# The first turn of the cross attention takes query tiles into the places of its missing output tiles, and the first keys are split sooner

## The chip, the cores and the metric

The kernel runs on one core of a Trainium2 chip. The metric is the device time of one execution in microseconds (us). Engines are named as the profile names them: PE is TensorE's matmul side (PEld its weight load), DVE is VectorE, ACT is ScalarE, POOL is GpSimd, SP is SyncE, which issues all DMAs here.

## The reference

One decoder layer on x (2 x 256 rows of 512) with a context (2 x 512 rows of 512): a causal self attention of 32 heads, a cross attention of 32 query heads over 8 key heads, and a permuted feed forward. The middle part is what the change touches:

```python
def _L0_xattn_ref(latents, context, Wq, Wk, Wv, Wo, q_norm_w, k_norm_w):
    kv = jnp.concatenate([context, latents], axis=1)
    q = (latents @ Wq).reshape(bsz, q_len, HEADS, HEAD_DIM).transpose(0, 2, 1, 3)
    k = (kv @ Wk).reshape(bsz, kv_len, KV_HEADS, HEAD_DIM).transpose(0, 2, 1, 3)
    v = (kv @ Wv).reshape(bsz, kv_len, KV_HEADS, HEAD_DIM).transpose(0, 2, 1, 3)
    q = rms_norm(q, q_norm_w)
    k = rms_norm(k, k_norm_w)
    qg = q.reshape(bsz, KV_HEADS, groups, q_len, HEAD_DIM)
    scores = jnp.einsum('bhgqd,bhkd->bhgqk', qg, k) * scale
    probs = jax.nn.softmax(scores.astype(jnp.float32), axis=-1).astype(q.dtype)
    out = jnp.einsum('bhgqk,bhkd->bhgqd', probs, v)
    ...
    return out @ Wo
x = _layernorm(x + _L0_attn_ref(x, ...), axis=-1)
x = _layernorm(x + _L0_xattn_ref(x, ctx_4096, ...), axis=-1)
x = _layernorm(x + _L0_ffn_ref(x, ...), axis=-1)
```

## The kernel before

Every product is made in three passes (`three_passes`): each operand is split into a rounded high part and the remainder, the low part, and hi x hi, hi x lo and lo x hi are added in one PSUM bank. Splitting a tile is therefore a copy (hi, mostly on ACT) and a difference (lo, on DVE or POOL), and both are awaited before the product.

**Stage 1, `self_attention_and_keys`.** The self attention and the keys and values of the cross attention, interleaved. `order_of_work` writes one list, ORDER, and every engine goes through it and does its own share of each entry. An engine never overtakes itself, so the list sets each engine's order. Entries that matter here: ("part", (n, r)) is an eighth of the key and value work for row tile n (12 of them); ("KT"/"KX") transposes of its keys and their way out; ("Q", a) is query tile a of head 0 (PE: 12 products, ACT: copy q_rows, DVE: four sums of squares); ("QT", a) its transpose and split; ("QM", (half, step)) the scale of two query tiles (step 0: mean on DVE, power on POOL; step 1: q_rms on DVE); ("W", 9) the split of the query weights of the next head, in four pieces; ("KS", 0) the split of head 0's first keys, in two halves; ("XS", j) score tile j of the first unit (PE), ("XM", j) its maximum (DVE), ("XE", j) its exponential (ACT), ("XI", j) 1 / sum (DVE) and the norm of the probabilities (POOL). XS 0 waits for both halves of KS.

**Stage 2, `cross_attention`.** Eight turns, one for each key head: the first one, five in a loop, and the last two written out. A turn has four segments s = 0 to 3. In segment s the engines work on unit s's probabilities (two batches x two pairs of query groups) and on the scores of the next unit: six transposed probability tiles T 0 to 5 (PE), split on ACT and DVE, six products with the values (O), four score tiles S with maximum M, exponential E, 1/sum I and POOL's norm. `Turn.tensor_order`, `scalar_order` and `vector_order` write a segment out, and each has four places f[0] to f[3] for fillers: query tiles Q of the next head, transposed query tiles QT, output tiles W of a finished head. On PE, f[0] and f[1] stand between T 1 and T 2, f[2] and f[3] between O 3 and O 4. T, Q, QT and W use three PSUM banks in rotation (4, 5, 6): a tile may only start when the tile three uses earlier has been taken out by DVE (`ring_free`). The table FILLERS says what stands where. In the first turn there is no finished head, so `fillers` drops the W entries of segment 0 (`from_before`), and two of its places are empty. In the last turn (LAST_FILLERS) no Q is left. POOL does the norms and the splits of keys, values and weights in the order of `body`; T 0 of a segment needs the norm of all four tiles of its unit.

Of the kernel before, what the change touches and what calls it, by code (L numbers as in the profile page):

```python
# [52 lines left out]
def f32(ap):  # L53
    return ap.bitcast(F32)
# [27 lines left out]
def order_of_work():  # L82
# [73 lines left out]
    order += [("Q", 2), ("QT", 1)]  # L156
# [3 lines left out]
    order += [("W", 9), ("QM", (1, 0))]  # L160
    parts(1)
    order.append(("KS", 0))
    parts(1)
    for j in range(UT):
        order.append(("XS", j))
        parts(1)
        if j == 0:
            order.append(("QM", (1, 1)))
        order.append(("XM", j))
        if j > 0:  # L170
            order.append(("XI", j - 1))
        order.append(("XE", j))
# [10 lines left out]
def self_attention_and_keys(nc, d, k):  # L183

    with ExitStack() as ctx:
# [165 lines left out]
        def _(pool):  # L351
# [44 lines left out]
            for what, a in ORDER:  # L396
# [22 lines left out]
                elif what == "W" and a == 9:  # L419
                    for i in range(KT):  # L420
                        pool.wait_ge(w_his, KT * a + i + 1)
                        nc.gpsimd.tensor_tensor(k.wq_lo[:, i, :], w_raw[:, i, :], f32(k.wq_hi[:, i, :]), ALU.subtract)\
                            .then_inc(k.wq_split, 1)
                elif what == "XI":
                    pool.wait_ge(k.rinv_made, a + 1)
                    nc.gpsimd.tensor_scalar(k.prob[:, a, :], k.prob[:, a, :], k.rinv[:, a:a + 1], 1.0, ALU.mult, ALU.mult)\
                        .then_inc(k.prob_made, 1)
                elif what == "LN":
                    pool.wait_ge(var_made, a + 1)
                    nc.gpsimd.tensor_tensor(rstd[:, a:a + 1], var[:, a:a + 1], minus_half[:, 0:1], ALU.pow)\  # L430
                        .then_inc(rstd_made, 1)

        @block.scalar
        def _(act):
# [75 lines left out]
            for what, a in ORDER:  # L510
# [13 lines left out]
                elif what == "W":  # L524
# [6 lines left out]
                    if a == 9:  # L531
                        act.wait_ge(q_ps, TT)
                    for i in range(KT):
                        weights_hi(a, i)
                elif what == "A":
# [412 lines left out]

LAST_FILLERS = ((("W", 2), ("QT", 2), ("QT", 3), None),
# [5 lines left out]
class Turn:  # L955
# [25 lines left out]
    def fillers(self, s):  # L981
        kept = []
        for f in (FILLERS if self.more else LAST_FILLERS)[s]:
# [39 lines left out]
def cross_attention(nc, d, k):  # L1023
# [7 lines left out]
    with ExitStack() as ctx:  # L1031
# [126 lines left out]
        def _(pool):  # L1158
# [46 lines left out]
            def body(turn):  # L1205
# [7 lines left out]
                if turn.first:  # L1213
                    norms(0, (0, 1))
                    keys(1, 0, 0, 0)
                    norms(0, (2,))
                    keys(1, 1, 0, 1)
                    norms(0, (3,))
# [23 lines left out]
                if turn.more:  # L1242
# [5 lines left out]
                    if turn.ahead:  # L1248
                        wait_alone(ring_full, turn.use[3, "Q", 3] + 1)
                        query_weights(0, i + 2, c + 12)  # L1250
# [615 lines left out]
```

## Time and profile before

| | us |
|---|---|
| median of 3 runs (865.48 to 865.60) | 865.54 |
| the profiled execution | 865.81 |
| its span, first to last instruction | 864.0 |
| busy in the span: PE / PEld | 828.4 / 696.8 |
| busy in the span: DVE / ACT / POOL | 548.3 / 475.1 / 524.4 |
| mean granted clock of TensorE | 0.991 of full speed |

The profiled execution is one of its own and its span begins and ends at instructions; 1.8 us lie around it. A time on the trace is counted from the start of the span. Stage 1 ends at about 287, the first turn of stage 2 runs from there to 354.5, and the last turn's segments 1 and 2 lie around 777 to 806. In a timeline a row's second number is the length of an instruction, or of a run of like ones (x4). Products are pipelined: the next may start before the length shown has gone by. A bracket at a row's end gives how long the engine stood idle before it and who released it.

### The profile page before, as it was taken

To read this page: it belongs to the slowest core of one execution; us is meant where nothing else is said; L and a number is where in the kernel's file an instruction comes from. 1 tells how busy PE (TensorE), PEld (TensorE's weight loads), DVE (VectorE), ACT (ScalarE), POOL (GpSimd) and SP (SyncE) were. 2 spreads that over 40 slices of the span, in tenths; PEclk is the share of its full clock that TensorE was granted. 3 is DMA by queue.
4 is the path that set the end of the run, shared out by engine and by line. 5 is a ranking of instruction groups with operands and counts; after the bars stand their busy time and mean duration, and the time that the engine had idled before them with its cause. 6 is when DMAs were issued, how large, how long until landed. Compare 5 with 4: busy or idle time off the path is not lost. (4 is left out here: it accounts for less than half of the span.)

```text
span 864.0 us, 15103 instructions
## 1 busy us (share of the span) xinstructions
PE 828.4 (96%) x4841; PEld 696.8 (81%) x4841; DVE 548.3 (63%) x1505; ACT 475.1 (55%) x1006; POOL 524.4 (61%) x676
## 2 busy tenths in 40 slices
PE   7999999899999899999999999999999999999976
PEld 5777777677887688888888888888888888888763
DVE  4376665656445667767676776667677767767543
ACT  5666663565345645555555555556555545555363
POOL 3576873676425476666756756775775676446831
PEclk9999999999999999999999999999999999999998
DMA  7604222121141532102112121121121102000011
GB/s 225 185 30 134 63 87 94 53 74 50 49 135 50 170 103 87 50 20 86 46 40 67 36 67 67 36 67 67 36 67 67 36 11 71 1 0 2 0 25 49
DMA packets 48510, 56.22 MB, mean 65 GB/s; under 512 B 4670, under 2 KB 29772, under 8 KB 48460
## 3 DMA queue, kind: packets, MB, share of 16 engines
q1 hardware_dynamic: 48460, 55.59, 20.9%
q8 instruction: 27, 0.44, 0.2%
q14 instruction: 23, 0.19, 0.1%
HBM read 41.95 MB, written 13.63 MB: 64 GB/s over the span
## 5 line engine op out<-in xcount | busy, mean ns | idle before, releaser
L1202 POOL TENSOR_SCALAR prob<-prob,x_rinv 128x768 f32<-128x768 f32 x124 | 113.1, 912 | 175.7 <-DVE x_rinv L1368 175.7
L1310 ACT ACTIVATE pT_hi<-bank 128x512 fp32r<-128x512 f32 x192 | 114.4, 598 | 93.8 <-PE bank L1500 92.7
L1293 ACT ACTIVATE prob<-bank,x_nm,q_rms 128x768 f32<-128x768 f32 x124 | 123.3, 994 | 46.1 <-DVE x_nm L1362 45.8
L1402 DVE TENSOR_TENSOR pT_lo<-bank,pT_hi 128x512 fp32r<-128x512 f32 x192 | 130.3, 680 | 6.9 <-ACT pT_hi L1310 5.4
L1359 DVE TENSOR_REDUCE x_mx<-bank 128x1 f32<-128x768 f32 x124 | 118.3, 954 | 22.8 <-PE bank L1463 22.4
L1500 PE MATMUL bank<-ident,prob 128*128 128x128 f32 x768 | 115.7, 273 | 4.3 <-POOL prob L1202 2.9
L1500 PEld LDWEIGHTS bank<-ident,prob 128*128 128x128 f32 x768 | 95.1, 141 | 16.6 <-POOL prob L1202 3.6
L48 PE MATMUL bank<-pT_hi,xv_hi 128*128 128x512 f32 x192 | 86.5, 450 | 0.9 <-DVE pT_lo L1402 0.8
L448 ACT ACTIVATE s_self<-s_self,nm_self 128x128 f32<-128x128 f32 (+1 forms) x128 | 57.0, 447 | 54.2 <-DVE nm_self L588 54.0
L50 PE MATMUL bank<-pT_hi,xv_lo 128*128 128x512 f32 x192 | 75.7, 394 | 0.0
L49 PE MATMUL bank<-pT_lo,xv_hi 128*128 128x512 f32 x192 | 75.2, 392 | 0.0
L1463 PE MATMUL bank<-xk_hi,qT_hi 128*128 128x384 f32 x244 | 66.0, 352 | 1.1 <-ACT prob L1293 1.0
L1463 PE MATMUL bank<-xk_lo,qT_hi 128*128 128x384 f32 x244 | 63.2, 340 | 0.0
L1463 PE MATMUL bank<-xk_hi,qT_lo 128*128 128x384 f32 x244 | 62.9, 338 | 0.0
L48 PE MATMUL bank<-wq_hi,x_hi 128*128 128x512 f32 x144 | 58.5, 406 | 0.0
L48 PE MATMUL bank<-w_hi,cT_hi 128*128 128x512 f32 x128 | 56.0, 438 | 1.2 <-DVE x_rows L672 1.2
L1319 ACT ACTIVATE oT_hi<-bank 128x512 fp32r<-128x512 f32 x32 | 19.2, 598 | 68.9 <-PE bank L50 68.9
L50 PE MATMUL bank<-wq_hi,x_lo 128*128 128x512 f32 x144 | 56.4, 392 | 0.0
L49 PE MATMUL bank<-wq_lo,x_hi 128*128 128x512 f32 x144 | 56.4, 391 | 0.0
L603 DVE COPY pT_self<-bank 128x384 f32<-128x384 f32 x64 | 35.3, 552 | 30.7 <-PE bank L810 30.5
L48 PE MATMUL bank<-wo_hi,oT_hi 128*128 128x512 f32 x128 | 51.9, 406 | 0.0
L1463 PEld LDWEIGHTS bank<-xk_hi,qT_hi 128*128 128x128 f32 x244 | 43.8, 190 | 9.8 <-ACT prob L1293 2.0
(216 smaller groups left out, 2050.3 us busy)
## 6 DMA issues: line engine op xcount, KB each, us to landing
wo_raw<-in_Wo SPq DMA_DIRECT2D x8, 1024.0 KB, 5.5
v_by_head<-v_st SPq DMA_DIRECT2D x12, 512.0 KB, 3.3
kT_by_head<-kT_st SPq DMA_DIRECT2D x12, 512.0 KB, 3.2
xk_raw<-kT_by_head SPq DMA_DIRECT2D x16, 384.0 KB, 3.2
xv_raw<-v_by_head SPq DMA_DIRECT2D x16, 384.0 KB, 3.2
wq_raw<-in_Wq SPq DMA_DIRECT2D x6, 1024.0 KB, 5.4
wq_raw<-in_w_attn SPq DMA_DIRECT2D x12, 256.0 KB, 3.9
xk_raw<-in_ctx SPq DMA_DIRECT2D x8, 256.0 KB, 2.6
```

The lines of the kernel that those rows point to most:

```text
L48: nc.tensor.matmul(out, a_hi, b_hi, start=first, stop=False)
L49: nc.tensor.matmul(out, a_hi, b_lo, start=False, stop=False)
L50: return nc.tensor.matmul(out, a_lo, b_hi, start=False, stop=last)
L448: nc.scalar.activation(s_sb[:, c % 2, i, a:e], s_sb[:, c % 2, i, a:e], ACT.Exp, bias=nm[:, c % 2, i, qt:qt + 1], scale=-1.0, accum_out=rsu ...
L603: nc.vector.tensor_copy(pT[:, c % 2, i, :], bank[:, bank_of("T", (c, i)), 0:3 * P]).then_inc(pt_out, 1)
L1202: nc.gpsimd.tensor_scalar(prob[:, s, :], prob[:, s, :], rinv[:, s:s + 1], 1.0, ALU.mult, ALU.mult)\
L1293: nc.scalar.activation(prob[:, s, :].rearrange("p (a e) -> p a e", a=2), bank[:, at:at + 2, 0:HALF], ACT.Exp, bias=nm[:, s:s + 1], scale=q ...
L1310: nc.scalar.activation(pT_hi[:, a, :], bank[:, turn.bank[s, what, a], :], ACT.Copy)\
L1359: nc.vector.reduce_max(mx[:, s:s + 1], bank[:, at:at + 2, 0:HALF], AX.XY)\
L1402: nc.vector.tensor_tensor(pT_lo[:, a, :], bank[:, turn.bank[s, what, a], :], f32(pT_hi[:, a, :]), ALU.subtract).then_inc(ring_out, 1)
L1463: last = nc.tensor.matmul(bank[:, at + c, 0:HALF], a_hi[:, g, w], k_part[:, b, c * HALF:(c + 1) * HALF], start=start, stop=stop)
L1500: last = nc.tensor.transpose(bank[:, at, j * P:(j + 1) * P], prob[:, UT * (s % 2) + j, a * P:(a + 1) * P], ident[:])
```

## The change

Three things are moved; no work is added or removed.

1. In ORDER, ("KS", 0) goes from behind the weights to behind ("QT", 1). ("W", 9) becomes eight entries: ("WH", i), ACT's copy of piece i, and ("WL", i), POOL's difference of piece i, spread over the following parts. ("QM", (1, 0)) stands ahead of them.
2. The first turn gets a table of its own, FIRST_FILLERS. Q 0 and Q 1 go to segment 0, Q 2 to segment 1, Q 3 to segment 2; the last place of segment 1 and the first of segment 3 become empty.
3. In the first turn POOL splits the keys of the second batch directly behind the first norm and does the other three norms after them.

```diff
@@ order_of_work
-    order += [("Q", 2), ("QT", 1)]
+    order += [("Q", 2), ("QT", 1), ("KS", 0)]
     parts(1)
     order += [("Q", 3), ("QM", (0, 1))]
     parts(1)
-    order += [("W", 9), ("QM", (1, 0))]
+    order += [("QM", (1, 0)), ("WH", 0), ("WH", 1)]
     parts(1)
-    order.append(("KS", 0))
+    order += [("WH", 2), ("WL", 0), ("WL", 1), ("WH", 3)]
     parts(1)
     for j in range(UT):
         order.append(("XS", j))
         parts(1)
         if j == 0:
-            order.append(("QM", (1, 1)))
+            order += [("QM", (1, 1)), ("WL", 2), ("WL", 3)]
@@ the first turn's table
+FIRST_FILLERS = ((("Q", 0), ("QT", 2), ("QT", 3), ("Q", 1)),
+                 (("Q", 2), None, None, None),
+                 (("Q", 3), ("QT", 0), ("QT", 1), ("W", 0)),
+                 (None, None, None, ("W", 1)))
...
-        for f in (FILLERS if self.more else LAST_FILLERS)[s]:
+        for f in (FIRST_FILLERS if self.first else FILLERS if self.more else LAST_FILLERS)[s]:
@@ POOL's body of a turn
                 if turn.first:
-                    norms(0, (0, 1))
+                    norms(0, (0,))
                     keys(1, 0, 0, 0)
-                    norms(0, (2,))
                     keys(1, 1, 0, 1)
-                    norms(0, (3,))
+                    norms(0, (1, 2, 3))
                     values(1, 0, i, c)
...
-                        wait_alone(ring_full, turn.use[3, "Q", 3] + 1)
+                        wait_alone(ring_full, turn.use[2 if turn.first else 3, "Q", 3] + 1)
```

**ScalarE near the end of stage 1**, from the copy of query tile 3 (q_rows) on; xk_hi is KS, wq_hi the weights, v_st, kT_st, k_rows and k_sq the parts of rows 10 and 11. Before:

```order
L546 ACTIVATE q_rows<-bank 128x512
L470 ACTIVATE v_st<-bank 128x512
L437 ACTIVATE wq_hi<-wq_raw 128x512 x4
L462 ACTIVATE kT_st<-bank,nw 128x512
L555 ACTIVATE xk_hi<-xk_raw0 128x384 x2
L478 ACTIVATE k_rows<-bank 128x512
L483 ACTIVATE k_sq<-k_rows 128x512
L462 ACTIVATE kT_st<-bank,nw 128x512
L560 ACTIVATE prob,x_rsum<-bank,x_nm,q_rms 128x768
```

After:

```order
L549 ACTIVATE qT_hi<-bank 128x4x128
L555 ACTIVATE xk_hi<-xk_raw0 128x384 x2
L546 ACTIVATE q_rows<-bank 128x512
L469 ACTIVATE v_st<-bank 128x512
L436 ACTIVATE wq_hi<-wq_raw 128x512 x2
L461 ACTIVATE kT_st<-bank,nw 128x512
L436 ACTIVATE wq_hi<-wq_raw 128x512 x2
L477 ACTIVATE k_rows<-bank 128x512
L482 ACTIVATE k_sq<-k_rows 128x512
```

The two halves of xk_hi moved ahead of the copy of query tile 3 and of the weights, and the weights stand in two pairs.

**GpSimd at the same place**: q_inv is the power of QM, wq_lo the weights, k_inv and k_rows the key norm of a part, prob the first norm of probabilities. Before:

```order
L422 TENSOR_TENSOR wq_lo<-wq_raw,wq_hi 128x512 x4
L418 TENSOR_TENSOR q_inv<-q_ms,minus_half 128x8
L411 TENSOR_TENSOR k_inv<-k_ms,minus_half 128x4
L413 TENSOR_TENSOR k_rows<-k_rows,k_inv 128x512
L426 TENSOR_SCALAR prob<-prob,x_rinv 128x768
```

After:

```order
L418 TENSOR_TENSOR q_inv<-q_ms,minus_half 128x8
L421 TENSOR_TENSOR wq_lo<-wq_raw,wq_hi 128x512 x2
L411 TENSOR_TENSOR k_inv<-k_ms,minus_half 128x4
L413 TENSOR_TENSOR k_rows<-k_rows,k_inv 128x512
L421 TENSOR_TENSOR wq_lo<-wq_raw,wq_hi 128x512 x2
L425 TENSOR_SCALAR prob<-prob,x_rinv 128x768
```

The power q_inv moved ahead of the weights, and two of the four weight pieces stand behind the key norm.

**ScalarE at the start of the first turn**, from the first two transposed tiles (pT_hi) to the output of segment 0 (oT_hi). Before:

```order
L1310 ACTIVATE pT_hi<-bank 128x512 x2
L1293 ACTIVATE prob,x_rsum<-bank,x_nm,q_rms 128x768
L1286 ACTIVATE qT_hi<-bank 128x4x128
L1310 ACTIVATE pT_hi<-bank 128x512 x2
L1293 ACTIVATE prob,x_rsum<-bank,x_nm,q_rms 128x768
L1310 ACTIVATE pT_hi<-bank 128x512
L1293 ACTIVATE prob,x_rsum<-bank,x_nm,q_rms 128x768
L1310 ACTIVATE pT_hi<-bank 128x512
L1293 ACTIVATE prob,x_rsum<-bank,x_nm,q_rms 128x768
L1286 ACTIVATE qT_hi<-bank 128x4x128
L1319 ACTIVATE oT_hi<-bank 128x2x256
```

After:

```order
L1313 ACTIVATE pT_hi<-bank 128x512 x2
L1296 ACTIVATE prob,x_rsum<-bank,x_nm,q_rms 128x768
L1285 ACTIVATE q_rows<-bank 128x512
L1289 ACTIVATE qT_hi<-bank 128x4x128
L1313 ACTIVATE pT_hi<-bank 128x512 x2
L1296 ACTIVATE prob,x_rsum<-bank,x_nm,q_rms 128x768
L1313 ACTIVATE pT_hi<-bank 128x512
L1296 ACTIVATE prob,x_rsum<-bank,x_nm,q_rms 128x768
L1313 ACTIVATE pT_hi<-bank 128x512
L1296 ACTIVATE prob,x_rsum<-bank,x_nm,q_rms 128x768
L1289 ACTIVATE qT_hi<-bank 128x4x128
L1285 ACTIVATE q_rows<-bank 128x512
```

Query tile 0 (q_rows) now stands behind the first exponential and ahead of QT 2 (qT_hi), query tile 1 ahead of oT_hi. VectorE's sums of squares stand in the same places.

**GpSimd in segment 0 of the first turn.** Before:

```order
L1202 TENSOR_SCALAR prob<-prob,x_rinv 128x768 x2
L1172 TENSOR_SCALAR xk_hi<-xk_raw1 128x384
L1174 TENSOR_TENSOR xk_lo<-xk_raw1,xk_hi 128x384
L1202 TENSOR_SCALAR prob<-prob,x_rinv 128x768
L1172 TENSOR_SCALAR xk_hi<-xk_raw1 128x384
L1174 TENSOR_TENSOR xk_lo<-xk_raw1,xk_hi 128x384
L1202 TENSOR_SCALAR prob<-prob,x_rinv 128x768
```

After:

```order
L1206 TENSOR_SCALAR prob<-prob,x_rinv 128x768
L1176 TENSOR_SCALAR xk_hi<-xk_raw1 128x384
L1178 TENSOR_TENSOR xk_lo<-xk_raw1,xk_hi 128x384
L1176 TENSOR_SCALAR xk_hi<-xk_raw1 128x384
L1178 TENSOR_TENSOR xk_lo<-xk_raw1,xk_hi 128x384
L1206 TENSOR_SCALAR prob<-prob,x_rinv 128x768 x3
```

The two key pieces now stand directly behind the first norm and ahead of the other three.

## Rows read from the trace of the kernel before

**Rows 1.** TensorE's timeline before the first score tile: start us, length us, engine, line

```profile
268.65 0.40 PE L50 MATMUL bank<-w_hi,x_lo 128*128 128x512 f32 x1
...
270.87 0.59 PE L926 MATMUL bank<-xk_hi,qT_hi 128*128 128x384 f32 x2 [1.82 <-issue]
```

**Rows 2.** Windows: busy us of PE, PEld, DVE, ACT, POOL; granted clock; DMA

```profile
272.00:276.00 4.00, 4.00 (x15) 3.41 (x14) 1.34 (x3) 1.70 (x4) 3.52 (x3) 0.58 0.29 92
...
303.00:307.00 4.00, 4.00 (x16) 3.71 (x16) 2.20 (x4) 1.57 (x3) 3.75 (x6) 0.61 0.94 331
...
791.00:796.00 5.00, 4.57 (x31) 4.13 (x30) 3.22 (x6) 3.08 (x6) 2.69 (x3) 1.00 0.00 0
```

**Rows 3.** Timelines of four engines around the first keys; their load's landing

```profile
252.11 0.35 SPq L341 DMA_DIRECT2D xk_raw<-kT_by_head  x1
...
DMA to landing us min/median/max: 3.2/3.2/3.2
...
264.49 0.60 ACT L546 ACTIVATE q_rows<-bank 128x512 f32<-128x512 f32 x1 [3.48 <-PE bank L50]
...
268.11 0.94 ACT L555 ACTIVATE xk_hi<-xk_raw 128x384 fp32r<-128x384 f32 x2
...
269.57 0.63 ACT L483 ACTIVATE k_sq<-k_rows 128x512 f32<-128x512 f32 x1
...
266.17 5.74 POOL L422 TENSOR_TENSOR wq_lo<-wq_raw,wq_hi 128x512 fp32r<-128x512 f32 x4 [6.65 <-ACT wq_hi L437]
...
268.67 2.10 DVE L707 TENSOR_TENSOR xk_lo<-xk_raw,xk_hi 128x384 fp32r<-128x384 f32 x2 [2.33 <-ACT xk_hi L555]
```

**Rows 4.** TensorE's timeline in segment 0 of the first turn

```profile
288.48 0.60 PE L1453 MATMUL bank<-ident,q_rows 128*128 128x128 f32 x4
...
289.80 0.66 PE L1500 MATMUL bank<-ident,prob 128*128 128x128 f32 x4 [0.72 <-DVE pT_lo L1402]
...
291.51 0.66 PE L1500 MATMUL bank<-ident,prob 128*128 128x128 f32 x4 [0.36 <-DVE pT_lo L1402]
...
296.07 0.62 PE L1463 MATMUL bank<-xk_hi,qT_hi 128*128 128x384 f32 x2 [1.02 <-ACT prob L1293]
...
302.74 0.48 PE L1500 MATMUL bank<-ident,prob 128*128 128x128 f32 x1 [2.04 <-POOL prob L1202]
```

**Rows 5.** Timelines: ScalarE in segment 0, VectorE's sums in segment 1

```profile
290.89 0.99 ACT L1293 ACTIVATE prob<-bank,x_nm,q_rms 128x768 f32<-128x768 f32 x1 [1.43 <-DVE x_nm L1362]
...
309.54 0.29 DVE L1333 CUSTOM_DVE_ANT_0 q_sq<-bank,q_rows 128x128 f32<-128x128 f32 x1 [1.74 <-ACT q_rows L1282]
...
310.38 0.08 DVE L1333 DVE_READ_ACCUMULATOR2_ANT q_ss<- 128x1 f32 x1
```

**Rows 6.** Timelines of SyncE and GpSimd in segment 0 of the first turn

```profile
290.11 0.35 SPq L1104 DMA_DIRECT2D xk_raw<-kT_by_head  x1
...
298.34 1.01 POOL L1174 TENSOR_TENSOR xk_lo<-xk_raw,xk_hi 128x384 fp32r<-128x384 f32 x1
...
301.78 0.91 POOL L1202 TENSOR_SCALAR prob<-prob,x_rinv 128x768 f32<-128x768 f32 x1
```

**Rows 7.** TensorE's timeline in segments 1 and 2 of the last turn

```profile
786.95 0.52 PE L1463 MATMUL bank<-xk_hi,qT_hi 128*128 128x384 f32 x2
...
791.87 0.33 PE L1500 MATMUL bank<-ident,prob 128*128 128x128 f32 x1 [0.43 <-POOL prob L1202]
...
799.29 0.61 PE L1463 MATMUL bank<-xk_hi,qT_hi 128*128 128x384 f32 x2
```

**Rows 8.** TensorE's timeline in segment 3 of the first turn

```profile
337.95 0.60 PE L1500 MATMUL bank<-ident,prob 128*128 128x128 f32 x4
...
339.80 0.48 PE L48 MATMUL bank<-wq_hi,x_hi 128*128 128x512 f32 x1
...
342.64 0.60 PE L1500 MATMUL bank<-ident,prob 128*128 128x128 f32 x4
...
348.15 0.52 PE L1463 MATMUL bank<-xk_hi,qT_hi 128*128 128x384 f32 x2
```

More of the change, by code:

```diff
@@ L418, in _ @@
                     nc.gpsimd.tensor_tensor(k.q_inv[:, w], k.q_ms[:, w], minus_half[:, w], ALU.pow).then_inc(k.first_inv, 1)
[L419 to L423, printed above, removed]
+                elif what == "WL":
+                    pool.wait_ge(w_his, KT * 9 + a + 1)
+                    nc.gpsimd.tensor_tensor(k.wq_lo[:, a, :], w_raw[:, a, :], f32(k.wq_hi[:, a, :]), ALU.subtract)\
+                        .then_inc(k.wq_split, 1)
                 elif what == "XI":
@@ L530, in _ @@
                         act.wait_ge(y_ps, TT)
-                    if a == 9:
-                        act.wait_ge(q_ps, TT)
                     for i in range(KT):
                         weights_hi(a, i)
+                elif what == "WH":
+                    act.wait_ge(q_ps, TT)
+                    weights_hi(9, a)
                 elif what == "A":
```

## The prediction, made before the changed kernel was run

> **What bounds the kernel now.** I read the granted clock and busy shares first, then TensorE's own list of waits, then its timeline around each wait, and then the timelines of the engines that release it. TensorE is the bound: it is busy without a gap through the middle turns of the second stage, so a microsecond of TensorE time that is saved ahead of them arrives at the end whole. The places where it stands still and that the change touches are two. At the end of the first stage it waits once, before the first score tile XS 0, from 268.65 + 0.23 = 268.88 (a 512-wide product starts every 0.23 us though it is shown 0.39 long) to 270.87, which is 1.99 us [rows 1]. In the first turn of the cross attention it waits four times: 0.72, 0.36, 1.02 and 2.04 us in the brackets [rows 4]. A bracket counts from the modelled end of the instruction ahead, so the loss is larger by its tail (0.25, 0.16, 0.16 and 0.13): 0.97, 0.52, 1.18 and 2.17, in sum 4.84 us. Behind the two longest waits the clock was half: 0.58 granted over 272 to 276 and 0.61 over 303 to 307, which costs 4 x 0.42 = 1.7 and 4 x 0.39 = 1.6 us [rows 2]. So 1.99 + 1.7 + 4.84 + 1.6 = 10.1 us are at stake, and no product, transpose or copy is added or taken away.
>
> **Part 1, the first keys are split earlier.** XS 0 waits for two halves of the key split. ScalarE did its two copies (0.94 us) at 268.11, behind four copies of the query weights; VectorE took 2.10 us for the two differences from 268.67 to 270.77 and TensorE started 0.10 later [rows 1, 3]. In the change the pair stands behind the split of query tile QT 1. Are the keys there? Their load was issued at 252.11 and took 3.2 us, so they lie in the buffer at 255.3 [rows 3]. Is there room? ScalarE sat idle for 3.48 us until 264.49 [rows 3], from 261.0, and 0.94 us fit; VectorE, idle as long before the sums of Q 3, can do its part by 263.2 (at 0.56 each, the length of the faster one in the 2.10) or 264.0 (at 2.10). Both are 5 us ahead of 268.88, so the 1.99 us go. GpSimd was busy from 266.17 for 5.74 us with the weights' low parts, beside which the 2.10 fell [rows 3].
> The Trainium skill, page "SBUF — State Buffer", section on contention of the shared port pair, says that a VectorE operation with two SBUF inputs and a GpSimd operation block each other for a whole instruction; the 2.10 us for a pair agree with it, and by it the pair would take 1.1 at its new place, where GpSimd is idle. Both values leave the sum as it is.
>
> What is late next? XS 1 follows XS 0 after one part of row 11, XS 2 needs the first exponential. VectorE first has to finish the row's sum of squares, whose squares ScalarE writes until 270.2 [rows 3] (so about 271.1), and the query scale, for which GpSimd's power now stands ahead of the weights and ends at 268. The maximum of XS 0 then runs at 271.3, its exponential at 272.6, and with 1.1 us from an exponential's start to the released product (0.99 for itself [rows 5], 0.1 to be seen) XS 2 may start at 273.7; TensorE comes there at 274.2. So 0.5 us is left, and a small miss costs tenths. On GpSimd the weight pieces WL 0 and 1 end at 270.5, the key norm of part 3 at 273.2, WL 2 and 3 (1.3 each) at 275.8, the first probability norm at 276.7 and the key norm of part 5 at 278.9, with TensorE asking for it at about 280.9. The weights are wanted only in the second stage. I cost all of this at nothing; without this cover WL 2 and 3 would cost up to 2.6. With no wait the clock should stay whole: it fell behind the two waits of about 2 us and was 1.00 around one of 0.43 in the last turn [rows 2, 7]. Part 1 gives 1.99 + 1.7 = **3.7 us**, with 1.9 as the low end (the clock falls anyway).
>
> **Part 2, query tiles in the places left empty in segment 0.** A query tile is 12 products, 342.64 - 339.80 = 2.84 us [rows 8]. Q 0 now stands between the second and third transposed tile of segment 0, Q 1 at its end. I follow it on the clock of the trace before, from the same entry. T 0 and T 1 end at 288.48; Q 0 runs to 291.3, QT 2 to 291.65. T 2 needs T 1's bank, free at 291.45, and starts at once: the waits of 0.97 and 0.52 go. T 3 now needs the bank of Q 0. ScalarE copies Q 0 behind the exponential (290.89 to 291.9) until 292.5, and VectorE's four sums of squares follow: from 309.54 they took until 310.47 [rows 5], 0.93 us, and begin 0.64 us after the copy's start. So Q 0's bank is free at 293.45, and TensorE, through with O 0 at 292.75, waits **0.7**. The next score tile behind the exponentials waits about **0.1** in place of 1.18, since the query tile has filled the time. Then Q 1 stands ahead of O 4 and O 5: segment 1 begins at 303.8, or 16.2 us after its entry. GpSimd by then has done one norm, two key pieces and three norms; the last exponential's sum is ready at about 300.8, its norm (0.91) at 301.8 [rows 6]. The 2.17 and the 1.6 of half clock go. Segments 0 and 1 lost 4.84 + 1.6 = 6.4 us, and now lose 0.8.
>
> **Part 3, what the later segments lose.** Q 2 keeps a place in segment 1 and Q 3 one in segment 2; the end of segment 1 and the front of segment 3 are empty. The trace shows both holes in its last turn, which has them by its own table. End of segment: from the last score tile at 786.95 to the fourth transpose at 791.87 it was 4.92 us, where the same work in segment 0, without its wait and its query transposes (0.35), took 302.74 - 296.07 - 2.17 - 0.35 = 4.15 and began 0.1 slow behind a wait of its own [rows 4]. So 4.92 - 4.05 = **0.9** is lost; the clock stayed whole [rows 2, 7]. The bracket alone (0.43 and a tail of 0.13) is the low end, 0.6. Front of segment 3: in the last turn the last score tile came 799.29 - 791.87 = 7.42 us after the fourth transpose, against 348.15 - 337.95 - 2.84 - 0.26 = 7.10 in segment 3 itself, less its query tile and three transposes [rows 7, 8]: 0.3 is the low end. In turn 0 the query scale stands ahead of T 0's difference on VectorE, and the second maximum stands behind the third tile's difference. The nearest row from above is the wait of 1.18 for such an exponential in segment 0 [rows 4]. I take **0.9**, since this wait has the same chain of VectorE and ScalarE. What follows, one output tile, covers the segment's last norm.
>
> The first turn now loses 0.7 + 0.1 + 0.9 + 0.9 = 2.6 instead of 6.4: **3.8 us** gained (3.0 to 4.5). Loads move with the GpSimd work that frees their buffers; every buffer is asked for later than that. The next turn's query weights no longer wait for Q 3 in segment 3, and GpSimd ends them some 5.8 us after that turn begins, 11 us before it needs a norm.
>
> **The sum.** The profiled execution took 865.81 us, its span is 864.0, so 1.8 lie around it. 864.0 - 3.7 - 3.8 = 856.5, and with 1.8 it is 858.3. The median of the three runs is 0.27 below the profiled run: **858.1 us**, a ratio of 0.991.
>
> **The rivals.**
> - *Half clock comes back elsewhere.* Waits of 0.7, 0.9 and 0.9 remain, and everything behind moves by 7.5 us against the clock's own course. Two rows at half clock cost 1.6 to 1.7 each [rows 2]. One gives 859.8, two 861.4. Against it: the wait of segment 1's kind left the clock at 1.00 [rows 2]. Chance 0.14.
> - *A new chain eats the first stage's gain.* If XS 2 or the key norms behind WL 2 and 3 come late, up to 2.6 of the 3.7 returns: 860.7. For it: only 0.5 us of room at XS 2. Chance 0.06.
> - *The holes only move.* If the two emptied places cost what segment 0 lost (1.18 and 2.17) and the new bank wait for Q 0 is 1.5, the first turn loses 4.9 + 1.6 of half clock and gains nothing: 858.1 + 3.8 = 861.9. The last turn speaks against it [rows 7]. Chance 0.05.
> - *Early keys aren't early.* Had their load landed after 262, ScalarE would stand at the copy with Q 3 and the row's values behind it. They lie there at 255.3 [rows 3]; then nothing of part 1 is gained, 861.8. Chance 0.01.
> - *Slower than before.* GpSimd now waits for head 0's second keys ahead of norms 1 to 3. Two pieces (0.5 + 1.01 each) and three norms of 0.91 make 5.8 us [rows 6], and segment 1 wants the last norm at 303.8, so each microsecond that the load lands after 298.0 goes to the end. It eats the whole gain from 298.0 + 7.5 = 305.5. Such a load took 3.2 us [rows 3] and here is issued at 290.11 [rows 6]. At 308 it would give 865.5 + 2.5 and half clock behind it, 869.7. Chance 0.02.
>
> **How the numbers follow.** The forecast has 0.72, its own range 856.6 to 859.5 from the bounds 3.0 to 4.5 and tenths at XS 2. The range of 856.2 to 861.6 leaves out about 0.1. A difference of 0.2% (1.7 us) is what a measurement of this kernel can tell from none, so the bounds are 863.8 and 867.3: faster 0.94 (forecast, half clock, chain, holes, with a little taken off for several at once), same 0.04, slower 0.02.
>
> **What would show it.** No wait before XS 0 and a granted clock of 1.00 from 268 to 287; the second stage beginning 3.7 us earlier (about 283.9); a wait of some 0.5 in the bracket before the fourth transposed tile of segment 0, on VectorE's sum of squares; none at segment 1's first transposes; one of 0.4 at segment 2's on GpSimd's norm, and short ones in segment 3 on VectorE or ScalarE; segment to segment, 16.2, 14.9, 17.4 and 14.6 us; the second turn beginning at about 347. A clock below 1.00 in the first turn, or a wait of over 1.5 us anywhere in it, would make it wrong.

## The result, and the profile of the changed kernel

| us | before | changed |
|---|---|---|
| median of 5 runs each | 865.60 (865.48 to 866.25) | 861.36 (859.09 to 861.86) |
| ratio, with its 95% interval | | 0.9939 (0.9916 to 0.9962) |
| the profiled execution | 865.81 | 861.36 |
| its span | 864.0 | 859.5 |
| PE busy in the span | 828.4 | 828.3 |
| first product of the columns (start of the program) | 13.98 | 15.31 |
| XS 0 could start | 268.88 | 271.81 |
| second stage begins | 287.57 | 286.82 |
| second turn begins | 354.45 | 349.93 |

The change gained 4.2 us where 7.4 were forecast; 861.36 lies inside the range of 856.2 to 861.6, 0.24 below its upper end. The surprise is in the last rows of the table: the changed places gave what was forecast, and 2.93 us were already lost before the first of them, in a part of the program that is the same in both kernels.

TensorE's timeline of the changed kernel at the end of the first stage (start us, length us, engine, line; the last row is the entry of the second stage):

```profile
271.81 0.51 PE L926 MATMUL bank<-xk_hi,qT_hi 128*128 128x384 f32 x2
...
274.68 0.51 PE L926 MATMUL bank<-xk_hi,qT_hi 128*128 128x384 f32 x2
...
277.10 0.51 PE L926 MATMUL bank<-xk_hi,qT_hi 128*128 128x384 f32 x2
...
286.82 1.06 PE L1503 MATMUL bank<-ident,prob 128*128 128x128 f32 x8 [0.32 <-PEq L185]
```

No bracket stands at XS 0 to 2. From XS 0 to the entry it is 15.01 us, against 18.69 of before from where XS 0 could start. That is 3.68 of the 3.7 of part 1. The two halves of the keys, in the timelines of ScalarE, VectorE and GpSimd, with the first exponential:

```profile
263.80 0.94 ACT L555 ACTIVATE xk_hi<-xk_raw 128x384 fp32r<-128x384 f32 x2
...
264.92 1.02 DVE L707 TENSOR_TENSOR xk_lo<-xk_raw,xk_hi 128x384 fp32r<-128x384 f32 x2
...
273.61 0.96 DVE L712 TENSOR_REDUCE x_mx<-bank 128x1 f32<-128x768 f32 x1
...
274.86 0.99 ACT L560 ACTIVATE prob<-bank,x_nm,q_rms 128x768 f32<-128x768 f32 x1 [0.68 <-DVE x_nm L714]
...
269.34 1.64 POOL L418 TENSOR_TENSOR q_inv<-q_ms,minus_half 128x8 f32<-128x8 f32 x1 [6.91 <-DVE q_ms L698]
```

VectorE's pair of differences took 1.02 us where GpSimd was idle (it is idle for the 6.91 us ahead of q_inv); in [rows 3] it took 2.10 beside GpSimd's weights. By the Trainium skill, page "SBUF — State Buffer", on the shared port pair, the two engines block each other for a whole instruction there; both durations agree with it.

The first turn, TensorE's timeline, all its rows that have a bracket after the entry, and the starts of segments 1 and 3 and of the second turn (x4 of L1503 with no bracket at 303.03, 335.29 and 349.93):

```profile
292.73 0.66 PE L1503 MATMUL bank<-ident,prob 128*128 128x128 f32 x4 [0.53 <-DVE q_ss L1336]
...
303.03 0.60 PE L1503 MATMUL bank<-ident,prob 128*128 128x128 f32 x4
...
318.14 0.33 PE L1503 MATMUL bank<-ident,prob 128*128 128x128 f32 x1 [0.43 <-POOL prob L1206]
...
335.29 0.60 PE L1503 MATMUL bank<-ident,prob 128*128 128x128 f32 x4
...
343.55 0.61 PE L1466 MATMUL bank<-xk_hi,qT_hi 128*128 128x384 f32 x2 [0.26 <-ACT prob L1296]
...
349.93 0.60 PE L1503 MATMUL bank<-ident,prob 128*128 128x128 f32 x4
```

The four brackets of [rows 4] (0.72, 0.36, 1.02, 2.04) are gone, and three shorter ones stand there. The turn takes 349.93 - 286.82 = 63.11 us, against 354.45 - 287.57 = 66.88 before. GpSimd has done the last norm of segment 0 in good time, although the second keys stand ahead of it:

```profile
292.67 0.51 POOL L1176 TENSOR_SCALAR xk_hi<-xk_raw 128x384 fp32r<-128x384 f32 x1 [0.17 <-DMA xk_raw<-kT_by_head]
...
300.19 0.91 POOL L1206 TENSOR_SCALAR prob<-prob,x_rinv 128x768 f32<-128x768 f32 x1 [0.33 <-DVE x_rinv L1371]
```

Windows (columns as in [rows 2]; the granted clock is the third number from the end) of the changed kernel: the end of the first stage, the first turn, and the place of [rows 2]'s second row:

```profile
268.00:287.00 19.00, 18.68 (x100) 16.34 (x99) 9.22 (x29) 12.36 (x24) 14.31 (x13) 1.00 0.28 84
287.00:349.00 62.00, 60.50 (x336) 52.01 (x335) 45.81 (x118) 37.19 (x69) 40.97 (x48) 1.00 0.36 117
303.00:307.00 4.00, 4.00 (x24) 3.58 (x23) 3.86 (x10) 2.06 (x4) 3.75 (x6) 1.00 0.36 98
```

**Where 2.9 us went.** The first product of the columns (L766) starts 1.33 us later than before. Up to there TensorE's products run at half pace (0.63 long, one every 0.43 us) until 12.4 in the kernel before and until 15.2 in the changed one. Of the 1.33 us, 0.2 are there at the first of these products (9.93 against 9.72) and 1.1 come from the longer stretch at half pace. This is the same product in the two timelines, of before and of the changed kernel:

```profile
12.42 0.47 PE L48 MATMUL bank<-x_hi,w_hi 128*128 128x512 f32 x1
```

```profile
12.62 0.63 PE L48 MATMUL bank<-x_hi,w_hi 128*128 128x512 f32 x1
```

Then, at 164 to 166, TensorE waits for VectorE's difference of x, as it does before. These are the rows of the changed kernel, and its windows there:

```profile
165.81 1.08 PE L839 MATMUL bank<-ident,k_rows 128*128 128x128 f32 x4 [1.78 <-DVE x_lo L681]
```

```profile
166.00:168.00 2.00, 2.00 (x8) 1.71 (x8) 0.93 (x5) 1.56 (x5) 1.59 (x4) 0.50 0.59 184
168.00:170.00 2.00, 2.00 (x20) 1.17 (x18) 0.00 (x0) 0.57 (x1) 1.83 (x6) 0.70 0.00 0
```

And those of the kernel before:

```profile
164.44 0.63 PE L839 MATMUL bank<-ident,k_rows 128*128 128x128 f32 x4 [1.78 <-DVE x_lo L681]
```

```profile
166.00:168.00 2.00, 2.00 (x38) 1.13 (x41) 0.78 (x5) 1.72 (x3) 1.83 (x6) 1.00 0.00 0
168.00:170.00 2.00, 2.00 (x27) 1.41 (x19) 0.48 (x1) 1.35 (x5) 1.83 (x6) 1.00 0.00 0
```

The wait is the same 1.78 us. Behind it the clock is at its lower level (0.50 is 1.2 of 2.4 GHz) in one and whole in the other, and from the transposes of x ahead of it (L898) to the second key transposes behind it (L839) it is 10.99 us against 9.39. So 1.3 and 1.6 of the 7.45 us that the changed places gave (3.68 and 3.77) were given back ahead of the change; 864.0 - 7.45 + 2.93 = 859.5, the span. What had to be found out: does the changed program make its own start slow, or does this fall out anew in each run of either kernel?

### The profile page after: what moved, and what is told of

It reads as the page before. It is cut to its first block and busy times, and to the rows that moved or that the text cites. A ratio compares the mean times of both kernels' runs of the same rounds, so it can differ in the third digit from the quotient of the medians.

```text
span 859.5 us, 15106 instructions
## 1 busy us (share of the span) xinstructions
PE 828.3 (96%) x4841; PEld 695.9 (81%) x4841; DVE 546.7 (64%) x1505; ACT 474.5 (55%) x1006; POOL 522.2 (61%) x676
## 5 line engine op out<-in xcount | busy, mean ns | idle before, releaser
L1503 PE MATMUL bank<-ident,prob 128*128 128x128 f32 x768 | 114.9, 272 | 2.1 <-POOL prob L1206 1.3
L1503 PEld LDWEIGHTS bank<-ident,prob 128*128 128x128 f32 x768 | 94.7, 140 | 14.0 <-POOL prob L1206 2.0
```

Source lines behind the costliest of these rows:

```text
L1503: last = nc.tensor.transpose(bank[:, at, j * P:(j + 1) * P], prob[:, UT * (s % 2) + j, a * P:(a + 1) * P], ident[:])
```

## The experiments

All stretches are of TensorE, in us. "164" is from the transposes of x (L898) to the second key transposes (L839) behind the wait of 1.78; "to XS 0" from the first column product to where XS 0 could start; "XS 0 on" from there to the second stage; "rest" from the second turn to the end of the span. The last column is the difference of the medians against the kernel before on the same chip; the experiments ran on three chips.

| kernel | column product | 164 | to XS 0 | XS 0 on | first turn | rest | median (runs) | against before |
|---|---|---|---|---|---|---|---|---|
| before | 13.98 | 9.4 | 254.9 | 18.7 | 66.9 | 509.6 | 865.60 (5) | |
| changed | 15.31 | 11.0 | 256.5 | 15.0 | 63.1 | 509.6 | 861.36 (5) | -4.2 |
| after_again | 15.42 | 9.4 | 254.8 | 15.0 | 63.1 | 511.6 | 859.90 (6) | -7.1 |
| before_again | 13.74 | 10.9 | 256.3 | 18.7 | 66.9 | 509.5 | 867.02 (12) | 0.0 |
| p1_keys | 14.08 | 9.4 | 255.0 | 15.0 | 67.0 | 509.6 | 863.05 (12) | -4.0 |
| p2_fill | 15.17 | 9.4 | 254.9 | 17.1 | 63.2 | 510.7 | 862.36 (12) | -4.6 |
| ks_only | 15.10 | 10.8 | 256.3 | 16.4 | 65.3 | 509.5 | 862.66 (12) | -4.7 |
| pool_old | 13.84 | 10.9 | 256.7 | 15.0 | 63.1 | 509.7 | 860.17 (6) | -7.2 |
| hole_front | 13.44 | 9.4 | 254.8 | 15.0 | 63.1 | 509.7 | 860.70 (6) | -6.7 |
| halves | 13.95 | 9.4 | 254.9 | 15.0 | 61.5 | 509.2 | 857.91 (6) | -9.5 |
| halves_again | 13.57 | 11.0 | 256.6 | 15.0 | 61.5 | 509.2 | 857.17 (6) | -8.6 |
| kt_later | 14.96 | 8.9 | 254.7 | 15.0 | 61.5 | 509.8 | 857.58 (6) | -8.2 |
| after_third | 13.65 | 9.4 | 254.9 | 15.0 | 63.2 | 511.6 | 860.19 (8) | -5.6 |

The kernel before ran beside them: 867.00 (862.44 to 869.12, 29 runs) for after_again, before_again, p1_keys and p2_fill; 867.37 (860.79 to 869.12, 17 runs) for ks_only, pool_old, hole_front and halves; 865.75 (860.63 to 868.61, 13 runs) for the last three.

**The changed kernel again**, without an edit.

> The changed kernel once more, unchanged. Theory A: the changed places give their 7.4 us every time, and the rest of the difference to the forecast is half clock in stretches that the change doesn't touch (the start, and behind the wait of 1.78 us near 164), which falls out anew in each run. Then the second stage's first turn is again 63.1 us long (first transposes of turn 0 to those of turn 1) and the 15.0 us from the first score tile to the second stage again 15.0, while the first score tile may start anywhere from 268.9 to 271.8; times from 858 to 862. Theory B: the changed program is slower at its start for a reason of its own (its instructions lie elsewhere). Then the first score tile starts at 271.8 again, with half clock until 15.3 us and again behind 164, and the time is 861.4.

Its profile has the wait of 1.78 at 165.91 and the whole clock behind it: 9.4 us. XS 0 starts at 270.26, though the column product was as late as 15.42. The profiled execution took 861.84 us all the same, since its rest is 2.0 us longer (511.6), far behind the change. The median is 7.1 below before.

**The kernel before again**, without an edit.

> The kernel before once more. Theory A: its start and the wait near 164 vary in the same way, so the second stage's beginning may lie from 287.6 to 290.5, and times may go above 866; if all stay within 865.5 to 866.3, theory A has to say why. Theory B: 865.5 to 866.3 every time, half clock until about 12.4 us at the start and none behind 164.

This time the kernel before has the lower clock behind the wait at 164 (10.9 us), beside the two places of [rows 2]. A program with nothing changed goes through the stretch in 9.4 us once and in 10.9 another time, and so does the changed one. For the stretch at 164 the reading that the changed program is slower there by itself falls. For the first microseconds it falls only with the third profile of the changed kernel, whose column product starts at 13.65 (after_third), ahead of both of before.

**The first move alone**: the kernel before with the edits in the list of the first stage (and the loops of ScalarE and GpSimd that carry out WH and WL, not shown).

```diff
-    order += [("Q", 2), ("QT", 1)]
+    order += [("Q", 2), ("QT", 1), ("KS", 0)]
...
-    order += [("W", 9), ("QM", (1, 0))]
+    order += [("QM", (1, 0)), ("WH", 0), ("WH", 1)]
...
-    order.append(("KS", 0))
+    order += [("WH", 2), ("WL", 0), ("WL", 1), ("WH", 3)]
...
-            order.append(("QM", (1, 1)))
+            order += [("QM", (1, 1)), ("WL", 2), ("WL", 3)]
```

> Part 1 alone: first keys split sooner and weights piece by piece, the first turn as before. Both theories: no wait before the first score tile and full clock behind it, 15.0 us from there to the second stage where before had 16.7 from its late start (18.7 from where it could have started); the first turn 66.9 as before. Theory A: 3.7 us less than before when the clock elsewhere is alike, 862, up to 865 when not. Theory B: 3.7 less and the same loss as in the changed kernel if the start is to blame, 864.8.

XS 0 starts at 269.04 with no wait, the second stage 15.01 us later, and the first turn keeps its 66.95 us: 3.68 us in the trace; the ratio to before is 0.9961 (0.9943 to 0.9979).

**The first turn's table alone**: the kernel before with the other half. FIRST_FILLERS is the table of the change, and GpSimd's wait for query tile 3 names segment 2, as there (both not shown).

```diff
-        for f in (FILLERS if self.more else LAST_FILLERS)[s]:
+        for f in (FIRST_FILLERS if self.first else FILLERS if self.more else LAST_FILLERS)[s]:
...
-                    norms(0, (0, 1))
+                    norms(0, (0,))
...
-                    norms(0, (2,))
...
-                    norms(0, (3,))
+                    norms(0, (1, 2, 3))
```

> Parts 2 and 3 alone: query tiles in the places left empty, and the order of the second keys on GpSimd. The wait of 1.8 before the first score tile and the half clock behind it stay; the first turn 63.1 instead of 66.9. Theory A: 3.8 us less than before, 861.8, with up to 1.7 more or less by the clock elsewhere. Theory B: 864.7 if the start is to blame.

The first turn takes 63.17 us, from 66.88: 3.71. The ratio is 0.9955 (0.9936 to 0.9975). The medians of the two halves alone, 4.0 and 4.6, add up to 8.6 us, where both together gave 4.2 to 7.1: the medians vary by more than the stretches do. This profile has the same wait before XS 0 as [rows 1], and another clock behind it (timeline and window of TensorE):

```profile
272.01 0.59 PE L926 MATMUL bank<-xk_hi,qT_hi 128*128 128x384 f32 x2 [1.82 <-issue]
```

```profile
272.00:276.00 4.00, 3.99 (x22) 3.70 (x23) 2.29 (x5) 0.69 (x1) 3.92 (x4) 1.00 0.14 41
```

[rows 2] has 0.58 over 272 to 276 behind the same 1.82 (there XS 0 starts 1.1 us sooner). XS 0 on took 17.1 here and 18.7 before. So the half clock doesn't follow this wait in every run either.

**The keys moved, the weights left in their block.**

```diff
-    order += [("Q", 2), ("QT", 1)]
+    order += [("Q", 2), ("QT", 1), ("KS", 0)]
...
-    order.append(("KS", 0))
     parts(1)
```

> The kernel before with one entry moved: the split of the first keys (KS) behind query tile QT 1. The query weights keep their block of four pieces and GpSimd's power for the query scale stays behind them; the second stage is as before. Theory (the two parts of the first move need each other): TensorE finds no wait before XS 0, but the scale q_rms of the first exponential needs GpSimd's power, which stands behind 5.74 us of weights (begun at 264 to 266, so the power ends at 270 to 272 on the clock of before), so that the first exponential comes at 272 to 273 and XS 2, which needs its bank, waits 0.5 to 2 us. From XS 0 to the first transposed tile of the second stage 15.5 to 17 us in place of 15.0; from XS 0's possible start to the second stage 0.1 to 1.8 us less than before's 18.7. Rival (the early keys alone do it): no wait of over 0.3 us in the stretch and 15.0 us from XS 0 to the second stage. In both the first turn stays at 65.3 to 66.9 us, depending on whether half clock falls behind its long wait.

TensorE and GpSimd around the first exponential:

```profile
277.95 0.62 PE L925 MATMUL bank<-xk_hi,qT_hi 128*128 128x384 f32 x2 [1.12 <-ACT prob L559]
```

```profile
268.65 5.09 POOL L421 TENSOR_TENSOR wq_lo<-wq_raw,wq_hi 128x512 fp32r<-128x512 f32 x4 [6.66 <-ACT wq_hi L436]
273.70 1.64 POOL L417 TENSOR_TENSOR q_inv<-q_ms,minus_half 128x8 f32<-128x8 f32 x1
```

The wait before XS 0 goes and one of 1.12 us comes at XS 2, because GpSimd's power (q_inv), which the first exponential needs, stands behind all four weight pieces. XS 0 on is 16.4 us, inside the 15.5 to 17 that were expected; the other bound written there, 0.1 to 1.8 below 18.7, was missed (2.3), as the clock stayed whole. So of the first move's 3.7 us the order of the power and the weights is 1.4 (16.4 against 15.0). The second surprise is its first turn of 65.33 us: the wait is 2.06 there, the window behind it reads

```profile
303.00:307.00 4.00, 4.00 (x22) 3.52 (x23) 2.48 (x5) 2.28 (x4) 3.75 (x6) 1.00 0.96 336
```

against 0.61 in [rows 2]. 66.88 - 65.33 = 1.55 is what the lower clock costs in this turn. The median is 4.7 below before, more than that of the whole first move (4.0), while the trace puts 1.4 us less on this stretch: differences of this size can't be read from the medians.

**GpSimd's old order in the first turn.**

```diff
-                    norms(0, (0,))
+                    norms(0, (0, 1))
                     keys(1, 0, 0, 0)
+                    norms(0, (2,))
                     keys(1, 1, 0, 1)
-                    norms(0, (1, 2, 3))
+                    norms(0, (3,))
```

> The changed kernel with GpSimd's old order in the first turn (two norms, a key piece, a norm, a key piece, a norm, in place of one norm, two key pieces, three norms). Theory (GpSimd's order in the first turn is worth nothing now, since the query tiles give it the time): the last norm ends within 0.3 us of the start of segment 1 and the first turn takes 63.1 to 63.4 us (63.11 and 63.14 in the two profiles of the changed kernel); ratio to the changed kernel within 0.1%. Rival (the new order is needed): the last norm comes 0.5 us or more late, a wait of 0.5 to 1.5 at the fourth transposed tile of segment 1 on GpSimd, and the turn takes 63.6 to 64.6 us.

The last norm ran from 300.60 to 301.51, wanted at 301.76 (segment 1's start in this run), and the turn took 63.13 us. The third edit of the change gives nothing beside the second; it only widens the margin, from 0.25 to 1.9 us.

**The hole moved from the end of segment 1 to its front.**

```diff
-                  (("Q", 2), None, None, None),
+                  (None, None, None, ("Q", 2)),
```

> The changed kernel with query tile 2 moved from the front of segment 1 to its end. Theory (the two empty places are of one price, about 0.9 us each): the wait of 0.43 on GpSimd before the fourth transposed tile of segment 2 goes (0.5 to 0.9 us gained with its tail) and waits of 0.9 to 1.5 in sum appear among the second to fourth transposed tiles of segment 1 on VectorE or ScalarE; the first turn takes 63.1 to 63.7 us in place of 63.1. Rival (the hole at the front is free, since the engines are ahead there): no wait at the front and the turn takes 62.3 us. If the hole at the end is free, the turn takes 64.0 or more.

The wait on GpSimd at segment 2 is gone, a wait in segment 1 has come, and the turn is 346.38 - 283.29 = 63.09:

```profile
307.72 0.62 PE L1466 MATMUL bank<-xk_hi,qT_hi 128*128 128x384 f32 x2 [0.26 <-ACT prob L1296]
```

It is the row that segment 3 has in the changed kernel, with the same bracket. The waits of 0.9 to 1.5 us that were expected among the transposed tiles of segment 1 did not come; the loss is seen in the length of the turn, which stayed (63.09 against 63.11). Between the end and the front of segment 1 the hole has one price.

**No hole left**: query tile 3 goes to the end of segment 1, and the two output tiles of the first head are cut into halves of 6 products that fill front and end of segments 2 and 3 ("H" is such a half; the code that handles it is not shown).

```diff
-                 (("Q", 2), None, None, None),
-                 (("Q", 3), ("QT", 0), ("QT", 1), ("W", 0)),
-                 (None, None, None, ("W", 1)))
+                 (("Q", 2), None, None, ("Q", 3)),
+                 (("H", (0, 0)), ("QT", 0), ("QT", 1), ("H", (0, 1))),
+                 (("H", (1, 0)), None, None, ("H", (1, 1))))
```

> The changed kernel with no place left empty: query tile 3 moved to the end of segment 1, and the two output tiles of the first head (W 0, W 1) each cut into two halves of 6 products, which fill the front and the end of segments 2 and 3. Two more takings of a bank for VectorE (some 0.7 us each), no product more or less. Theory (the holes at the end of segment 1 and at the front of segment 3 cost 0.9 each, and half a tile, 1.4 us of TensorE, is enough to cover either): the waits of 0.43 on GpSimd at segment 2 and of 0.26 on ScalarE in segment 3 go, no new wait of over 0.2 appears, and the first turn takes 61.2 to 61.8 us in place of 63.1; the time is 1.5 to 1.9 us below the changed kernel's. Rival (half a tile is too short, the holes only spread): two or more waits of 0.4 to 0.9 at the places that now have a half, and the turn takes 62.4 to 63.5 us.

In the first turn one bracket is left after the entry (TensorE's timeline; the last row is the second turn):

```profile
283.82 1.06 PE L1506 MATMUL bank<-ident,prob 128*128 128x128 f32 x8 [0.32 <-PEq L185]
...
289.73 0.65 PE L1506 MATMUL bank<-ident,prob 128*128 128x128 f32 x4 [0.52 <-DVE q_ss L1335]
...
345.30 0.60 PE L1506 MATMUL bank<-ident,prob 128*128 128x128 f32 x4
```

The turn takes 61.48 us, 1.63 less than with the holes. By segments, counted from score tile to score tile and with 2.84 [rows 8] for the query tile that moved, segment 1 gains 1.17 and segment 3 gains 0.83, and segment 2, where two halves stand in place of two whole tiles, gives 0.35 back; from what was not looked into. The hole at the end of segment 1 was filled by a whole query tile and the one at the front of segment 3 by half an output tile, so half a tile is shown to take away the second one's 0.83. The median is 9.5 us below before, ratio 0.9893 (0.9864 to 0.9922).

**The same kernel again, beside the changed one**, both without an edit.

> The kernel with halves once more, word for word, beside the changed kernel on the same chip. Theory: XS 0 to the second stage 15.0, first turn 61.5; the median 1.6 us below the changed kernel's and 8.5 to 10 below before; what differs between its two profiles lies ahead of XS 0 (half clock at the start or behind the wait at 164) or behind 815. Rival (its lead of 2 to 3 us in the other comparison was chance): within 0.5 us of the changed kernel.

> The changed kernel once more, word for word. Theory: XS 0 to the second stage 15.0 and first turn 63.1, as in its other two profiles; XS 0 itself anywhere from 268.3 to 271.9, by how often half clock falls at the start and behind the wait at 164; median 6 to 8 us below before. Rival (the first comparison, 4.2 us, is the kernel's true gain): 3.5 to 5 us below before.

857.17 against 860.19 us: 3.0 apart. In all their runs together the kernel with halves has a median of 857.6 (12 runs, 854.9 to 860.5) and the changed kernel 860.2 (19 runs, 857.0 to 862.1). 1.6 of the 2.6 between them are in every trace; the remainder is of the size of what varies. The gain over before came out at 5.6, between the 3.5 to 5 of the rival and the 6 to 8 expected.

A third place outside the change varies too. Ahead of the last stage TensorE waits 3.33 or 3.34 us in each of the thirteen profiles, and in eleven the lower clock stands behind it; in both profiles of the kernel with halves it doesn't. These are the transposes behind that wait, of after_third and of halves (2.54 us long with the lower clock over a part of them, 1.94 at the whole one; up to 3.65 in p2_fill):

```profile
817.73 2.54 PE L1693 MATMUL bank<-ident,x_rows 128*128 128x128 f32 x16 [3.33 <-PEq L1035]
```

```profile
816.33 1.94 PE L1702 MATMUL bank<-ident,x_rows 128*128 128x128 f32 x16 [3.33 <-PEq L1034]
```

In eight profiles the clock is whole again within some 4 us and the rest is 509.5 to 509.8, against 509.2 in the two of the kernel with halves. In after_again and after_third it stays low until about 826 (0.50 to 0.73 over 818 to 826 in after_third), and the rest is 511.6; in p2_fill it is 510.7. That both profiles of the kernel with halves escaped may be chance; against the 509.5 to 509.8 it is worth 0.3 to 0.6 us.

**The wait at 164 filled.** The kernel with halves, and one swap far ahead of the change: the key transposes go behind the six products that followed them.

```diff
+    at = next(i for i in range(order.index(("XT", 1)), len(order)) if order[i][0] == "KT")
+    order[at], order[at + 1] = order[at + 1], order[at]
     return order
```

> The kernel with halves and one swap in the first stage, far ahead of the changed places: the key transposes that wait 1.78 us for VectorE's difference of x at about 164 stand behind the six products that followed them, so that these fill the wait. Theory (the half clock there comes of that wait and is not bound to any kernel): at most 0.4 us of wait is left, the granted clock is 1.00 between 160 and 176 in the profile, XS 0 starts 1.4 us or more earlier than in a kernel whose clock stayed whole there (268.3 to 268.8), so at 266.9 to 267.4 where the start also went at full clock; the stretches from XS 0 to the second stage (15.0) and the first turn (61.5) stay; the median lies 1.4 to 2.5 us below the kernel with halves. Rival (the swap only moves the wait, to the transposes or the product of the values that come next): the wait of 1.78 comes back within 10 us, the median stays within 0.5 us. If half clock is still found between 160 and 176 without a wait of over 0.6, it doesn't come of the wait.

TensorE's timeline and a window there:

```profile
165.63 0.63 PE L841 MATMUL bank<-ident,k_rows 128*128 128x128 f32 x4 [0.39 <-DVE x_lo L683]
...
171.24 0.63 PE L841 MATMUL bank<-ident,k_rows 128*128 128x128 f32 x4 [0.77 <-DVE x_lo L611]
```

```profile
166.00:168.00 2.00, 2.00 (x43) 1.24 (x45) 0.75 (x5) 1.87 (x6) 1.69 (x5) 1.00 0.51 158
```

The wait of 1.78 shrank to 0.39, and a new one of 0.77 came at the next key transposes, on VectorE's split of the value products: 1.39 saved, 0.93 given back with its tail. The stretch takes 8.9 us against 9.4 at the whole clock and 11.0 at the lower one. XS 0 was expected at 266.9 to 267.4 and came at 269.62. Of the 2.2 us between, 0.93 is the new wait with its tail, 1.0 the late start (14.96 against 13.95 in halves), and about 0.26 was lost between the stretch and XS 0 (254.7 against 254.9, only 0.2 of the 0.46 left). The median, 857.58, is within 0.5 us of that of halves on the same chip (857.17), so as a gain the rival was right. The six runs lie between 856.74 and 857.69; the twelve of the kernel with halves spread over 5.6 us, and four of them are faster than all six. The narrow spread fits the filled wait, but with one profile and six runs it is not shown that no lower clock falls there any more.

## Why the prediction was right and where it was not

- **Part 1, 3.7 us: right.** 3.68 in the changed kernel, and 3.68 alone. The room at XS 2 had been put too small: the first exponential began at 274.86, so XS 2 could be released at 275.96 (274.86 and 1.1), 1.1 us before TensorE came to it and not 0.5.
- **Parts 2 and 3, 3.8 us: right.** 3.77 in the changed kernel, 3.71 alone. The segments were forecast at 16.2, 14.9, 17.4 and 14.6 and took 16.21 (entry to 303.03), then from first score tile to first score tile 14.85, 17.42 and 14.64. The wait for query tile 0's bank was 0.53 and a tail, for 0.7. The two holes, put at 0.9 each, were 1.2 (end of segment 1) and 0.8 (front of segment 3) by the kernel that fills them.
- **GpSimd and the second keys: the slower rival fell.** The load was there at 292.7 and the last norm was done at 301.1, 1.9 us before it was wanted. That the order of the norms was changed at all gave nothing.
- **The sum, 864.0 - 3.7 - 3.8: here it failed.** The step took everything outside the changed places from one profiled execution as if it were fixed. It isn't: over thirteen profiles the first column product starts at 13.44 to 15.42; the wait of 1.78 at 164 is followed by the lower clock in 5 of the 12 that have it, for 1.4 to 1.6 us; the rest takes 509.2 to 511.6. The profile of before had the better side of the first two, and the changed kernel's had the worse, which is 2.9 of the 3.0 us between span and forecast (859.5 against 856.5). The same 2.9 us are why the second stage began at 286.82 and not at 283.9, and the second turn at 349.93 and not at 347, though the first stage's end and the first turn gave what was forecast.
- **The half clock behind the removed waits was taken as certain, 1.7 and 1.6.** It fell behind the wait before XS 0 in 2 of 3 profiles that have it (not in p2_fill) and behind the 2 us wait of the first turn in 3 of 4 (not in ks_only), and cost 1.6 us each time. So what the change surely takes out is the waits, 2.0 + 2.2 (65.33 to 63.13) = 4.2 us; the other 3.2 or so come only in the runs in which the clock would have fallen. The three comparisons of the changed kernel, 4.2, 7.1 and 5.6 us, lie in that band. Its fastest run of 19 is 3.6 us below the fastest of the 64 runs of before that stood beside the kernels (857.02 and 860.63), its slowest 7.1 below their slowest (862.05 and 869.12).
- **The rival that came nearest was "half clock comes back elsewhere"**, put at 0.14, and its reasons were wrong. It asked whether the short waits that remain would trip the clock; those of 0.26 to 0.53 left it at 1.00 in every profile. It also had everything behind the change move by 7.5 us, but what was lost lay ahead of the change: one place at the lower clock, behind the old wait at 164, and a start 1.3 us later. That its figure for two places, 861.4, is the time measured is luck. The forecast counted all the half clock in before's profile as gained and took the start as fixed; that the time still lay in the range, by 0.24 us, is luck too. [rows 2] alone could not tell: the profile of before showed two waits of 1.8 to 2.0 us with the lower clock behind them, and a third of 1.78 without, and that third one was not asked about. Nor was the wait of 3.34 ahead of the last stage, which had the lower clock behind it there too.

## What to carry to other kernels

Build a forecast's sum on what the two kernels differ in, and take for the untouched remainder the spread of several runs, not the one profile that happens to lie there; a difference below that spread is judged by stretches of the trace between two fixed instructions, which repeated here within about 0.1 us wherever the clock was the same in them (15.01 to 15.02 and 63.09 to 63.17 in the changed places), while the median of the unchanged kernel before moved by 1.8 between comparisons (865.6 to 867.4). A wait on the bounding engine has a sure price, its length, and, from 1.8 us up in this kernel, a second one that only some runs pay, the stretch at half clock behind it; list every wait of that length or longer in the profile, with what the clock did behind it, before one of them is priced. And when a place is left without filler work, half a tile (1.4 us of products) was enough to take its 0.8 us away, and the turn with all places filled was 1.6 us shorter; cutting two tiles that had covered their places whole may have cost the 0.35 us of segment 2, so cut only what is needed elsewhere.

## What the runs showed of the hardware

- The same wait of 1.78 us, in the same place, with the same work around it, was followed by the lower clock in 5 of 12 profiles, that of 1.82 before XS 0 in 2 of 3, that of 2.0 to 2.1 in the first turn in 3 of 4: 10 of 19, and each costs 1.4 to 1.6 us. The wait of 3.33 ahead of the last stage was followed by it in 11 of 13. Waits of 0.26 to 1.25 us between 140 and 350 (1.25 near 147, 1.22 or 1.23 twice between 190 and 215) were never followed by it. What decides between the runs stays open: the order of the work and the wait itself are the same in both cases.
  The Trainium skill, page "TensorE: Matmul & The Clock Gate", section "Part 1: The HAM clock gate", says that the monitor behind the clock runs free of the kernel's start, so that the same kernel can show different stretches at half clock. The 5 of 12 agree with that; no run here shows the monitor itself.
- At the start of the program products ran at half pace (0.63 us long) while the granted clock of the window was shown as 1.00 (over 12 to 14 in the changed kernel, where the product at 12.62 stands). In before_again, pool_old, halves_again and after_third the first products ran at the whole pace (0.39 long) and then fell to 0.63, and there the column shows 0.50; in the changed kernel they are slow from the first one on, and it shows 1.00. In the first microseconds the length of a product is the better witness. The window of the changed kernel:

```profile
12.00:14.00 2.00, 2.00 (x6) 1.52 (x6) 0.00 (x0) 0.00 (x0) 0.00 (x0) 1.00 0.85 269
```

- VectorE's pair with two inputs took 1.02 us with GpSimd idle and 2.10 beside it; GpSimd's four weight pieces took 5.74 us beside VectorE's pair and 5.09 in ks_only, where the pair lay elsewhere; in the changed kernel they took 2.54 and 2.55 for two each.
